# Queries' transfers in four parts, the last group's exponentials added on VectorE, and the last two half heads finished beside the output projection

## What is computed

```
x = x + 0.5 * ffn(layernorm(x))     # two shared experts + top 2 of 8 routed experts, SwiGLU, F = 352
x = x + attn(layernorm(x))          # 16 query heads, 4 key/value heads of 32, rotary, softmax over 1024 keys
x = x + 0.5 * ffn(layernorm(x))
```

## Time and profile before

| what | us |
|---|---|
| median of 3 runs (lowest to highest) | 1739.38 (1735.95 to 1741.07) |
| profiled execution, its own time | 1733.54 |
| its span from first to last instruction | 1731.7 |
| PE busy in the span | 1616.3 (93%) |
| DVE, ACT, POOL busy | 856.9, 657.7, 919.6 |

### The profile page before, as it was taken

The page is one execution under the profiler, slowest core; times in us unless marked ns, Lnnn a source line. Parts: engine busy times, 40 slices in busy tenths (PEclk is TensorE's granted clock), DMA queues, the critical chain, the costliest instruction groups (busy, mean ns, idle before and its releaser), DMA issues.

```text
span 1731.7 us, 24109 instructions
## 1 busy us (share of the span) xinstructions
PE 1616.3 (93%) x8356; PEld 1157.0 (67%) x8356; DVE 856.9 (49%) x1470; ACT 657.7 (38%) x974; POOL 919.6 (53%) x757
## 2 busy tenths in 40 slices
PE   6999999999998998999988999988999999999997
PEld 5778899999876753343333343424777889899985
DVE  5554322222576866666656666724655432222236
ACT  4422222323233254555554555663542222233220
POOL 3116674327459566567666576861222447631645
PEclk9999999999998989899888898999999999999998
DMA  9206553333552221111111111015101545433427
GB/s 349 98 29 224 218 180 125 133 130 125 164 165 76 58 56 28 27 28 28 38 33 28 26 27 28 12 28 161 55 1 67 186 158 181 172 125 120 143 84 244
DMA packets 89345, 180.15 MB, mean 104 GB/s; under 512 B 30225, under 2 KB 31121, under 8 KB 86929
## 3 DMA queue, kind: packets, MB, share of 16 engines
q1 hardware_dynamic: 76400, 104.95, 20.2%
q0 software_dynamic: 12832, 73.67, 12.0%
HBM read 106.48 MB, written 55.97 MB: 94 GB/s over the span
## 4 chain that ended last, share of the span: by engine, by line
PE 69%; DMA 10%; DVE 7%; POOL 5%; ACT 3%; SPq 3%; issue 3%; POOLq 0%; DVEq 0%; ACTq 0%
PE PS L1166 9%; PE PS L1168 9%; PE PS L1167 9%; PE PS L1399 7%; PE PS L1413 7%; PE PS L1380 6%; DMA xn<-x_routed 4%; SPq L1102 3%; PE PS L1429 2%; DMA xs<-x_routed 2%; PE PS L1303 2%; PE PS L1308 2%; PE PS L1306 2%; PE PS L1305 2%; PE PS L1307 2%
## 5 line engine op out<-in xcount | busy, mean ns | idle before, releaser
L1652 ACT ACTIVATE PT<-PS 128x1024 f32<-128x1024 f32 x256 | 258.7, 1025 | 207.9 <-PE PS L1399 206.9
L1949 DVE TENSOR_REDUCE nmf_later<-PS 128x1 f32<-128x1024 f32 x160 | 194.8, 1219 | 85.2 <-PE PS L1380 84.8
L1399 PE MATMUL PS<-QS,KS 98*128 98x512 f32 x512 | 192.2, 462 | 46.6 <-DVE nmf_later L1949 31.1
L967 POOL TENSOR_TENSOR added<-PT 128x1024 f32<-128x1024 f32 x60 | 145.7, 2429 | 161.0 <-ACT PT L1652 161.0
L1413 PE MATMUL PS<-PT,V 128*32 128x512 f32 x1024 | 219.3, 656 | 0.0
L1399 PEld LDWEIGHTS PS<-QS,KS 98*128 98x128 f32 x512 | 92.1, 206 | 180.6 <-DVE nmf_later L1949 77.4
L2017 POOL TENSOR_TENSOR W<-raw,W 128x544 fp32r<-128x544 f32 x144 | 190.2, 1355 | 1.5
L1380 PE MATMUL PS<-KS,QS 96*128 96x512 f32 x512 | 180.6, 437 | 3.6 <-DVE nmf_first L1949 1.6
L1916 DVE TENSOR_TENSOR thid<-thid,PS 128x352 f32<-128x352 f32 x78 | 40.7, 521 | 245.7 <-ACT thid L1583 245.7
L1422 PE MATMUL PS<-PT,ones 128*32 128x512 f32 x256 | 150.4, 673 | 0.0
L1166 PE MATMUL PS<-xh,W 128*128 128x512 f32 x352 | 141.0, 401 | 4.8 <-DVE hid L1827 2.0
(11 more groups left out here) (197 smaller groups left out, 3835.8 us busy)
## 6 DMA issues: line engine op xcount, KB each, us to landing
raw<-ffn_w POOLq DMA_DIRECT2D x18, 2176.0 KB, 10.3
y_routed<-ytile SPq DMA_DIRECT2D x78, 256.0 KB, 2.2
xn<-x_routed SPq DMA_DIRECT2D x40, 256.0 KB, 3.5
x_routed<-xq SPq DMA_DIRECT2D x1, 9984.0 KB, 29.4
xs<-x_routed SPq DMA_DIRECT2D x38, 256.0 KB, 3.7
QS<-later_hi SPq DMA_DIRECT2D x112, 64.0 KB, 2.0
raw<-ffn_w SPq DMA_DIRECT2D x6, 768.0 KB, 8.1
raw<-ffn_w SPq DMA_DIRECT2D x16, 272.0 KB, 4.3
```

The costliest lines, as they stand in the source:

```text
L967: e.tensor_tensor(to, PT[:, (u + 1) % PTBUF, :], PT[:, (u + 2) % PTBUF, :], ALU.add).then_inc(done.sem, 1)
L1399: mm = e.matmul(PS[:, i + j, :], KS[0:ROWS, b, g, kt * P:(kt + 1) * P], QS[n % 3][0:ROWS, h, hf * GRP:(hf + 1) * GRP], start=True, stop=True)
L1652: e.activation(PT[:, u % PTBUF, :], PS[:, i:i + 2, :].rearrange("p b n -> p (b n)"), ACT.Exp, scale=SCALE).then_inc(p_ready.sem, 1)
L1949: e.tensor_reduce(row_maxima(n)[:, h, t:t + 1], PS[:, i:i + 2, :].rearrange("p b n -> p (b n)"), AX.X, ALU.max, negate=True).then_inc(max_ ...
```

## The change

1. `place_queries` of groups 2 to 7 (`in_steps`) still splits the queries, but issues none of its 12 transfers on SP. A new item `queries_out` issues the 3 transfers of one head; four of them are put into the list at even units: after un 8 at un 10, 12, 14, 16, after un 24 at un 26, 28, 30 and 0 of the next group.
2. SP's part of `invert` ends with L1134. The wait for it and L1141 are a new item `inverse_back`, in pair 2 rather than pair 1.
3. `sums_on_vector` is true for all 8 half heads of the last group, not only for the four with hf = 1.
4. At the end, `store_head(62)` and `store_head(63)` move behind the third and the fifth tile's `project_out`, and half head 63's `invert`, `inverse_back` and `x_back` behind the first one's. No instruction is added or removed by any of this.

```diff
 def sums_on_vector(hh):
-    n, _, hf = half_head(hh)
-    return n == len(KV_GROUPS) - 1 and hf == 1
+    return half_head(hh)[0] == len(KV_GROUPS) - 1
+def in_steps(n):
+    return n >= 2
...
             work.append(("values", hh, 2))
+            if hh:
+                work.append(("inverse_back", hh - 1))
         if hh >= 0 and pair == 3:
             work.append(("sums_out", hh))
+        if queries and un % 2 == 0:
+            work.append(("queries_out", *queries.pop(0)))
...
             work.append(("place_queries", n + 2, un // (UNITS // 2)))
+            queries.extend((n + 2, un // (UNITS // 2), h2) for h2 in range(REP))
...
     work.extend([("sum", hh), ("values", hh, 0), ("invert", hh - 1), ("values", hh, 1), ("store_head", hh - 2),
-                 ("values", hh, 2), ("store_head", hh - 1), ("sums_out", hh)])
+                 ("values", hh, 2), ("inverse_back", hh - 1), ("sums_out", hh)])
...
-    last = [("invert", hh), ("store_head", hh), ("x_back",)]
+    last = {3: [("invert", hh), ("inverse_back", hh), ("x_back",)], 5: [("store_head", hh - 1)],
+            7: [("store_head", hh)]}
...
         if i < NT:
             work.append(("split_heads", turned[i]))
-        if i == 2:
-            work.extend(last)
+        work.extend(last.get(i, []))
         if i >= 2:
             work.append(("project_out", turned[i - 2]))
...
-                for h in range(REP):
+                for h in () if in_steps(n) else range(REP):
...
+            elif kind == "queries_out":
+                n, half, h = key
+                cols = slice(half * GRP, (half + 1) * GRP)
+                for i, part_ in enumerate(QUERY_STACK):
+                    e.dma_start(QS[n % 3][i * HD:(i + 1) * HD, h, cols].bitcast(F32),
+                                (later_hi, later_lo)[part_][h * HD:(h + 1) * HD, :]
+                                ).then_inc(queries_placed[n % 3].sem, 16)
...
                 e.dma_start(inverse_rows[hh % 2, :].rearrange("(p i) -> p i", i=TPG),
                             inverses[:, hh % 2, :]).then_inc(inverse_out.sem, 16)
+            elif kind == "inverse_back":
+                hh, = key
                 sp.wait_ge(inverse_out, hh)
```

More of the change, by code:

```diff
@@ L423, in order_of_work @@
     work.append(("heads_start",))
-    maxima, lows = [], []
+    maxima, lows, queries = [], [], []
     groups = len(KV_GROUPS)
@@ L879, in macaron @@
         elif kind == "invert":
-            for a in (inverted, inverse_out, inverse_in):
+            for a in (inverted, inverse_out):
                 a.plan(*key)
+        elif kind == "inverse_back":
+            inverse_in.plan(*key)
         elif kind == "wo":
```

## The result

| what | before | after |
|---|---|---|
| median of 4 runs (lowest to highest), us | 1739.33 (1735.95 to 1741.07) | 1642.35 (1639.02 to 1647.11) |
| ratio of the two, 95% interval | | 0.9447 (0.9416 to 0.9477) |
| profiled execution, own time and span, us | 1733.5, 1731.7 | 1644.7, 1642.9 |
| mean granted clock in it | 0.958 | 0.983 |

The change takes 97.0 us off the median; 101 were forecast (1739 to 1638). The lines moved: L1399 is now L1420, L1380 is L1401, L1949 is L1970, L1970 is L1991, the three steps of the row sums L1126, L1134, L1141 are L1145, L1153, L1162, the queries' L1102 is L1120, `place_low`'s L1109 is L1128, and L1422 is L1443.

What follows compares the result with a forecast made beforehand. PE bounds the kernel, through idle gaps by late row maxima and the slow clock behind them. Gains 83 + 11 + 6 = 100 us from the median 1739.4 give 1639, stated as 1638 us; range 1625 to 1666.

Steps and rivals of the forecast that it cites:

- The rival that the clock stays low: PEclk in the heads stays below 1 for another reason than the gaps; 1682 us, chance 5%.
- Change 1, 83 us: Half heads 2 to 47: 12 query-placement stalls cost 85.4 us; sending queries in four parts gains all but 2.
- The allowance of 2 us for what sticks out: Over the whole kernel, remaining DVE waits that still show on PE were put at 2 us, bounds 0 and 10.
- B's wait: DVE's wait for row sums at the second of three consecutive half heads of a placement: 0 to 0.8 us.
- C's: DVE's wait for row sums at the third of three consecutive half heads of a placement: 0.2 to 1.6 us.
- the first 1.17 us of a wait: In the heads, 1.17 us of each DVE wait is hidden from PE by the three pairs of banks.
- Change 3, 11 us: Last group's eight half heads: sums on DVE end PE's waits for POOL; 11 us taken, bounds 4 and 11.6.
- Changes 2 and 4, 6 us: End of the heads: without the store in the way the projection starts earlier; gain 4.5 to 6.7, taken as 6 us.
- The 4.5 us: Before the projection: DVE's split of the first tile is ready sooner, so PE starts 4.5 us earlier.
- The 2.2 us of clock: Start of the projection: if the shorter gap leaves the clock high, 4.36 us at half clock take 2.2 us.
- The covers: Projection: later read back of x, stores of half heads 62 and 63 and weight loads stay hidden, costing 0.
- Two smaller stalls for one: Rival in the heads: DVE waits 2 to 3 us, PE idles 24 x 1.3 = 31 us; 1668 us, chance 12%.

Runs made afterwards that it cites:

- `half_in_steps`: Changed kernel, but groups 5 to 7 send their queries in one go of 12 transfers again; 1692.28 us, 0.9676 of the kernel before.
- `q_alone`: Kernel before plus changes 1 and 2 only, queries' transfers in four parts; 1651.36 us, 0.9539 of the kernel before.
- `sums_alone`: Kernel before plus change 3 (with `inverse_back`), queries in one go and old end; 1722.66 us, 0.9953 of the kernel before.
- `tail`: Changed kernel, last group starting with another bank pair, first two tiles split earlier, POOL's Wo split after DVE's sums; 1649.69 us, 0.9441 of the kernel before.
- `end_alone`: Kernel before plus change 4 (with `inverse_back`), last stores and read back of x behind tiles; 1727.19 us, 0.9981 of the kernel before.
- `two_parts`: Changed kernel, but each placement's 12 query transfers go in two parts of 6; 1662.31 us, 0.9604 of the kernel before.
- `act_queue`: Changed kernel, but the transfers of `queries_out` are issued by ACT instead of SP; 1667.73 us, 0.9542 of the kernel before.
- `between`: Changed kernel, query parts issued between the reciprocals' store and read back, one per placement behind a sum; 1647.02 us, 0.9449 of the kernel before.
- `after_again`: The changed kernel, unaltered, run again on a second chip; 1650.72 us, 0.9449 of the kernel before.
- `after_third`: The changed kernel, unaltered, run once more on a third chip; 1648.99 us, 0.9464 of the kernel before.

## Why the prediction was right

- **What bounds the kernel** held: idle time of PE by late maxima, and the clock behind it. That the clock is given back was shown twice, by 1.00 from 640 to 1043 us in the kernel after and by `half_in_steps`. The rival that the clock stays low is out.
- **Change 1, 83 us:** 81.3 in the trace, 79.8 for `q_alone`. The allowance of 2 us for what sticks out was half of what it should have been: it was 4.1 us, of which 3.0 are idle time. B's wait was laid at 0 to 0.8 us and C's at 0.2 to 1.6; of the 14 waits ten are at most 1.63, the others 1.82, 2.09, 2.13 and 2.77. The term that was off is the landing of the store (L1134, now L1153), 3.35 us there where 2.0 to 2.8 were taken. That PE doesn't feel the first 1.17 us of a wait was on the safe side: 1.17 us is right for the stalls of before, but of each of the four waits that show after, 1.48 us were hidden. With 1.17 three more waits, of 1.35 to 1.63 us, would have shown as gaps.
- **Change 3, 11 us:** 10.0 in the trace, 8.5 (4.8 to 11.6 by the interval) for `sums_alone`. The half heads are at 5.44 to 5.50 us, as estimated from 5.51, but for two at 7.10 and 6.24. In the kernel after the clash with POOL happened, at two of four splits of Wo. 1.6 us were lost against the full 11.6. That full sum was itself short, since the last of the eight takes 4.99 us and not 5.51: with the two engines kept apart `tail` takes 43.1 us for the eight, so the clash cost 45.66 - 43.13 = 2.5 us in this execution, inside the 3.3 us that the prediction gave for it if all showed.
- **Changes 2 and 4, 6 us:** 4.4 in the trace, 3.9 for `end_alone`. The 4.5 us came as worked out up to the first project_out. The 2.2 us of clock did not, as PE still had gaps of 0.63 and 1.93 us and ran 3.4 us at half clock; in `two_parts`, `act_queue` and `between` the same two gaps cost no clock. And the sum left out that the products of the last two half heads (L1450, 2 matmuls in 1.04 us each time) now stand behind the first project_out instead of ahead of it. From OT(63) to the gap of 1.3 us behind the first transposes it is 29.9 us instead of 32.7 (1124.97 - 1095.08 and 1218.58 - 1185.91): 2.8 us are left of the 4.4. The covers held, in that PE waited neither for x nor for weights. But DVE waited for x at its first add, 5.10 us, and not at its fifth: that is the read back of the first four tiles (L1167), which goes once the last values are done and which the prediction didn't look at. The weights are loaded 22.0 us behind the first project_out instead of 6.1.
- **The sum:** 81.3 + 10.0 + 4.4 = 95.7 us up to the projection, against 100. Half head 54 to 55 took 9.06 us instead of 7.51, as half clock followed its gap of 1.32. From the first project_out to the end the profiled execution took 545.9 us where that of before took 539.5. Of these 6.4 us, 1.7 lie in the first 28 us (see above) and 3.6 in the last 19, in code that the change does not touch, with 15.6 us of half clock in the trace of after and 9.5 in that of before. The eight other profiled executions with the changed end took 540.2 to 545.2 us for the same work, the two others with the old end 541.2 and 541.7, so most of the 6.4 is scatter. So the profiled spans differ by 88.8 only, while the medians differ by 97.0; the profiled execution of before was faster than each of its four runs. On the two other chips the medians of the two kernels differ by 97.1 and 94.9 us: that the medians come so near the forecast 101 is not chance.
- **Two smaller stalls for one** did not come, but it was nearer than its 12% say: with twice the size of a part it is there (`two_parts`, 0.9604 of before, which would be 1670 us on the first chip, against that rival's 1668). It was right to let the range reach to it.

What stays open: what holds the store up at 739.21 (its neighbours, at 730.38 and 747.34, landed within 2.3 and 1.7 us). It goes behind six of the queries' transfers and the maxima's two, and at that place it took 3.5 us in `after_again` and `after_third` too, and 1.5 in `between`, where no queries' transfers stand right ahead of it. But of the ten stores of the changed kernel with the same eight right ahead of them, eight were read back 1.5 to 2.5 us later and two 3.3, and one with SP's queue idle for 3 us ahead of it took 3.3 us in `after_third`. So the transfers ahead of it are neither shown to be the cause nor ruled out. Open too is what decides whether a gap of 1.3 us costs clock.

## What to carry to other kernels

A batch of transfers in a strictly ordered queue costs its whole issue time (0.63 us each here) to every latency chain whose next step stands behind it; cut it so that what lies between two steps is shorter than the slack of the consumer, and best put each piece where the queue waits for a landing anyway (here that removed the last gaps, 2 us). Price a stall on TensorE as idle time plus the slow clock behind it: here 3.6 us idle cost 6.9. Moving issues to a queue whose engine computes isn't free, and the engine's own timeline shows it as idle time in front of its next instruction.

## What the runs showed of the hardware that was not expected

- **The length of a gap alone does not decide the clock.** Of the same gap of 1.32 us ahead of half head 55 the kernel after had 3.4 us of half clock (9.06 us for the half head), `after_again` and `after_third` none (7.51). In `two_parts` a gap of 1.37 us was followed by 3.4 us of half clock, and gaps of 2.06 and 2.08 us by none; gaps of 3.1 to 4.6 us were followed by between 3.4 and 10.2 us of it.
- **Three issues on ACT's queue took 1.8 us of ACT** (753.35 to 755.15), in which nothing but the OT begun before them ran.
- **What a late operand hides is not constant.** PE's gap was DVE's wait less 1.1 to 1.3 us in the 12 stalls of before, and less 1.48 us in the four that show after.
- **Both sides of a clash lose.** DVE's add was 0.96 us longer and POOL's 0.84, each having waited for the other in turn.
